# The first, the batch-change and the last steps of a pipelined fp32 block kernel in another order

## The reference

```python
x = x + layernorm(attn(layernorm(x)))     # long convolution, out projection, gated MLP
x = x + layernorm(ffn(layernorm(x)))      # two layers with weights changed per batch
# attn, its last part
y = (yconv + xv * D_skip) * x2
y = y @ out_proj_w.T + u
zm = rmsnorm(y, post_norm_w)
return y + gelu_tanh(zm @ l1_w.T) * (zm @ l2_w.T) @ l3_w.T       # 672 wide
# ffn: rows 1 to 16 of the batch make rank-one updates m1, m2 of W1 and W2
h = gelu(x @ W1.T + scale * (x @ m1.T) + b1)                     # 1024 wide
return h @ W2.T + scale * (h @ m2.T) + b2
```

## Time and profile before

| | us |
|---|---|
| median of three runs | 1096.37 |
| the profiled execution | 1095.71 |
| its span | 1093.9 |
| PE busy | 1063.1 (97% of the span) |
| DVE busy | 879.1 (80%) |
| ACT busy | 720.8 (66%) |
| POOL busy | 298.7 (27%) |

### The profile page before, as it was taken

How to read it: one execution, slowest core, us unless ns; L and a number is a source line. 1 busy time by engine, 2 the same in 40 slices (tenths; PEclk the granted TensorE clock), 3 DMA queues, 4 the chain that set the end, 5 groups by cost and what they waited for, 6 DMA issues and landing times.

```text
span 1093.9 us, 25039 instructions
## 1 busy us (share of the span) xinstructions
PE 1063.1 (97%) x9016; PEld 1007.7 (92%) x9016; DVE 879.1 (80%) x2313; ACT 720.8 (66%) x1613; POOL 298.7 (27%) x577
## 2 busy tenths in 40 slices
PE   8899999999999999999999999989999999999996
PEld 7777787778999999999999999989999999999996
DVE  7999998763788877888888777898888888877874
ACT  7878887664565666666666666665666666666553
POOL 6677784620001111112111111121112111111111
PEclk9999999999999999999999999999999999999999
DMA  3338988984642333333333333443333333333100
GB/s 127 117 126 229 270 229 219 400 312 59 147 73 40 59 60 49 59 49 50 52 55 63 56 59 49 109 105 50 50 59 49 51 53 57 65 59 49 31 11 30
DMA packets 113051, 104.93 MB, mean 96 GB/s; under 512 B 7600, under 2 KB 103792, under 8 KB 112672
## 3 DMA queue, kind: packets, MB, share of 16 engines
q1 hardware_dynamic: 111696, 100.77, 42.1%
q0 software_dynamic: 736, 2.51, 0.7%
q10 hardware_dynamic: 496, 0.05, 0.0%
HBM read 77.84 MB, written 32.80 MB: 101 GB/s over the span
## 4 chain that ended last, share of the span: by engine, by line
PE 63%; DVE 7%; issue 4%; POOL 1%; ACT 1%; DMA 0%; ACTq 0%; SPq 0%; DVEq 0%; POOLq 0%
PE ps_ring L1464 33%; PE ps_w L1464 14%; PE ps_m L1464 9%; PE ps_o L1464 4%; PE ps_rt L1479 2%; DVE base L1318 1%; POOL sc L1082 1%; DVE bn L1222 1%; PE ps_m L1529 1%; DVE prod L1265 0%; PE ps_w L1474 0%; DMA base<-in_w 0%; DVE ht_l L1234 0%; DVE pt_l L1234 0%; DVE x L1436 0%
## 5 line engine op out<-in xcount | busy, mean ns | idle before, releaser
L1082 POOL TENSOR_TENSOR sc<-sc,neg_half 128x2 f32<-128x2 f32 x128 | 95.5, 746 | 690.6 <-DVE sc L1417 407.8
L1142 ACT ACTIVATE gate<-ps_ring 128x256 f32<-128x256 f32 x192 | 73.0, 381 | 127.4 <-PE ps_ring L1464 126.6
L1163 ACT ACTIVATE hid<-ps_ring,b1s 128x256 f32<-128x256 f32 x256 | 112.4, 484 | 29.4 <-PE ps_ring L1464 9.3
L1464 PE MATMUL ps_ring<-mt_h,wl_h 128*128 128x256 f32 x640 | 125.8, 278 | 2.4 <-DVE prod L1265 1.3
L1464 PE MATMUL ps_ring<-mt_l,wl_h 128*128 128x256 f32 x640 | 125.7, 278 | 2.2 <-DVE mt_l L1234 2.2
L1464 PE MATMUL ps_ring<-mt_h,wl_l 128*128 128x256 f32 x640 | 125.0, 277 | 0.0
L1234 DVE TENSOR_TENSOR ht_l<-hid,ht_h 128x256 fp32r<-128x256 f32 x256 | 103.1, 423 | 16.0 <-ACT ht_h L1167 10.0
L1464 PE MATMUL ps_ring<-xt_h,we_h 128*128 128x256 f32 x512 | 103.2, 283 | 2.8 <-DVE prod L1265 2.4
L1265 DVE TENSOR_TENSOR prod<-ps_ring,gate 128x256 f32<-128x256 f32 x192 | 80.7, 420 | 24.9 <-ACT gate L1142 20.6
L1464 PEld LDWEIGHTS ps_ring<-mt_h,wl_h 128*128 128x128 f32 x640 | 96.6, 188 | 3.9 <-ACT mt_h L1211 2.2
L1464 PE MATMUL ps_ring<-xt_h,we_l 128*128 128x256 f32 x512 | 99.9, 276 | 0.0
(11 more groups left out here) (186 smaller groups left out, 2746.6 us busy)
## 6 DMA issues: line engine op xcount, KB each, us to landing
toep_scratch<-taps_scratch SPq DMA_DIRECT2D x30, 512.0 KB, 7.7
toep<-toep_scratch SPq DMA_DIRECT2D x30, 512.0 KB, 9.9
...
```

Source lines behind the costliest of these rows:

```text
L1082: nc.gpsimd.tensor_tensor(sc[:, to], sc[:, to], neg_half[:, 0, 0:CC], ALU.pow).then_inc(S[done], 1)
L1142: nc.scalar.activation(gate[rows_of, m % 2], ring[m % RING][rows_of, 0], ACT.Gelu_apprx_tanh).then_inc(S["gate_done"], 1)
L1163: nc.scalar.activation(hid[:, m % HIDS], block_of, ACT.Gelu, bias=b1s[:, m:m + 1]).then_inc(S["hid_done"], 1)
L1464: mm = nc.tensor.matmul(out, lhs(a, kk), rhs(b, kk), start=(j == 0), stop=(closed and j == len(todo) - 1))
```

## The change

The steps of the fill, of the batch change and of the end are put in another order on every engine:

- Unit 1's y and x2 are loaded at the start, into frow and hid, which are free then. DVE gates them at the end of step -1, ahead of step 0's products. PE runs unit 1's out projection behind the second block of step 0 and transposes its scaled rows ahead of step 0's `mlp_down`; ACT makes its squares and scaled rows between the gates. Unit 2's y is gated at the end of step 0, ahead of the sum of `mlp_down`.
- In steps 1 to 3, 18 and 19 (`relieved`) ACT makes the high parts of the fifth and sixth block and of the next unit's y, which DVE made before.
- Table loads are left out in steps 0 and 1, and come behind the high part of the transposed rows in steps -1, 2 and 18. The low part of the transposed rows comes sooner on DVE. The low parts of the last two pieces of the second weights move from one step's end into the next step's products.
- `mlp_down` is split, with `turn_scaled` between its halves in step 1. The tables of spare matmuls are smaller.
- SP loads the next batch's first weights ahead of the output's store.
- The last unit is finished in two chunks of 128 rows: each `ffn_down` half has its own PSUM tile and its own signal, the statistics, the power, one multiply-add and a store are made per chunk on DVE and POOL, without ACT. In the last two units `ffn_down` starts with six of the eight high parts there.

```diff
-    BEFORE_TURN = {0: (8, 7, 8, 6), 2: (0, 0, 0, 6), 3: (0, 5, 0, 4), 19: (0, 5, 5, 5)}
-    BEFORE_HIGH = {0: 9, 1: 10, 2: 10, 3: 9, 19: 9}
-    BEFORE_LOW = {1: 13, 2: 7, 3: 13, 19: 10}
-    BEFORE_DOWN = {0: (6, 6), 1: (4, 4)}
+    BEFORE_TURN = {0: (8, 7, 8, 6), 3: (0, 3, 0, 4), 19: (0, 5, 5, 5)}
+    BEFORE_HIGH = {0: 4, 3: 4, 19: 4}
+    BEFORE_DOWN = {0: (10, 7), 1: (0, 11)}
...
+        def bare(n):
+            return valid(n, UC) and not valid(n - FFN_AT, UC)
+        def exposed(n):
+            return bare(n) or (valid(n, UC) and late(n - FFN_AT))
+        def sooner(n):
+            return n == 1
+        def relieved(n):
+            return n in (1, 2, 3) or any(n == b * UCB + i for b in range(1, B) for i in (2, 3))
+        def highs(n):
+            return FB if relieved(n) else ACT_HIGHS
+        def highs_done(n, m):
+            return sum(highs(i) for i in range(n)) + m + 1
+        def highs_here(n, m):
+            return sum(FB - highs(i) for i in range(n)) + m - highs(n) + 1
+        def early(n):
+            return n == 2
+        def gated(n):
+            return hid[:, 0:KB] if sooner(n) else x2s[:]
...
+            load_y(1, frow, y_second)
+            sp.dma_start(gated(1), x2_dram[:, :, TC:2 * TC]).then_inc(x2_second, 16)
+            sp.wait_ge(S["yrow_done"], 1)
+            sp.dma_start(xa[:], x_rows[1]).then_inc(S["xa_in"], 16)
...
-                if valid(n + 2, UC):
-                    sp.wait_ge(S["yf_done"], n + 2)
-                    load_y(n + 2)
-                    sp.wait_ge(S["yl_done"], n + 2)
+                if valid(n + 2, UC) and not sooner(n + 2):
+                    last = 1 if sooner(n + 1) else n + 2
+                    sp.wait_ge(S["yf_done"], last)
+                    load_y(n + 2, yin, S["y_in"])
+                    sp.wait_ge(S["yl_done"], last)
...
+                if made:
+                    load_base1(made)
+                if w == LAST:
+                    for c in range(CC):
+                        sp.wait_ge(S["out_done"], w + c + 1)
+                        sp.dma_start(out_rows[w][:, c], xa[:, c]).then_inc(S["rows_out"], 16)
...
+                if m == FULL:
+                    nc.scalar.activation(pstack[REST:2 * REST], src, ACT.Copy).then_inc(S["stacked"], 1)
...
-                        if 0 < m < FB - 1:
+                        if 0 < m <= highs(n):
                             product_high(n, m - 1)
-                        if n == 0 and m == 3:
+                        if m == 2 and relieved(n) and valid(n + 1, UC) and not early(n + 1):
+                            gated_high(n + 1)
...
+                        if second is not None and m == 1:
+                            high_parts(second, (LORA + 1,))
                         if m in (2, 3) and valid(w, UC) and not late(w):
                             last_norm(w, m - 2)
-                    load_table(ACT.Gelu)
+                        if sooner(n + 1) and m == 2:
+                            squares(n + 1)
+                        if sooner(n + 1) and m == 4:
+                            scaled_rows(n + 1)
+                    if relieved(n):
+                        product_high(n, FULL)
+                    if valid(h, UC):
...
+                    if not sooner(n + 1):
+                        squares(n + 1)
+                        scaled_rows(n + 1)
+                    if valid(n, UC) and not exposed(n):
+                        load_table(ACT.Gelu_apprx_tanh)
...
+                    if not valid(n, UC) or (exposed(n) and not bare(n)):
+                        load_table(ACT.Gelu_apprx_tanh)
...
+            def last_chunks(w):
+                kept = x1[:, w % KEPT]
+                dve.wait_ge(S["a_mean"], w + 1)
+                for c in range(CC):
+                    nc.vector.tensor_scalar(kept[:, c], kept[:, c], mean_a[:, w % KEPT, c:c + 1], None, ALU.subtract
+                                            ).then_inc(S["x_bare"], 1)
+                for c, bank in enumerate((ps_w, ps_m)):
+                    dve.wait_ge(S["w2_mm"], w + c + 1)
+                    nc.vector.tensor_tensor(xa[:, c], bank[:, c], b2s[:], ALU.add).then_inc(S["f_done"], 1)
+                    dve.wait_ge(S["f_done"], w + c + 1)
+                    nc.vector.bn_stats(bn[:, 2, c], xa[:, c]).then_inc(S["f_stat"], 1)
+                    stats = 2 * (CC * w + c) + 1
+                    aggregate_after(dve, nc.vector, mark[:], S["f_stat"], stats)
+                    nc.vector.bn_aggr(mvf[:, c], bn[:, 2, c]).then_inc(S["f_stat"], 1)
+                    dve.wait_ge(S["f_stat"], stats + 1)
+                    nc.vector.tensor_scalar(sc[:, 2, c:c + 1], mvf[:, c, 1:2], EPS_LN, None, ALU.add
+                                            ).then_inc(S["f_var"], 1)
+                    nc.vector.tensor_scalar(xa[:, c], xa[:, c], mvf[:, c, 0:1], None, ALU.subtract
+                                            ).then_inc(S["f_bare"], 1)
+                    dve.wait_ge(S["f_bare"], c + 1)
+                    dve.wait_ge(S["x_bare"], CC)
+                    dve.wait_ge(S["f_scale"], w + c + 1)
+                    nc.vector.scalar_tensor_tensor(xa[:, c], xa[:, c], sc[:, 2, c:c + 1], kept[:, c],
+                                                   ALU.mult, ALU.add).then_inc(S["out_done"], 1)
...
+                if bare(n):
+                    turned_low(n + 1)
+                if early(n + 2):
+                    for part in range(3):
+                        gate_y(n + 2, part)
...
+                    if exposed(n) and not bare(n):
+                        turned_low(n + 1)
...
+                    if made == 0:
+                        up_weights(made, LORA // 2)
+                    elif made is not None:
+                        turned_low(n + 1)
+                    if first is not None:
+                        down_weights(first, LORA + 1, range(1))
...
+                    down_weights(first, LORA + 1, range(1, LORA))
...
+                if second is not None:
+                    low_part(second, LORA, "weight_low2")
...
+                if second is not None:
+                    low_part(second, LORA + 1, "weight_low2")
...
+                bank = ps_m if (h, c) == (LAST, CC - 1) else ps_w
+                highs_ready = ()
                 if c == 0:
-                    pe.wait_ge(S["hh_even"], HB // 2 * (h + 1))
-                    pe.wait_ge(S["hh_odd"], HB // 2 * (h + 1))
+                    behind = (HB - HIGHS_FIRST) // 2 if h >= LAST - 1 else 0
+                    pe.wait_ge(S["hh_even"], HB // 2 * (h + 1) - behind)
+                    pe.wait_ge(S["hh_odd"], HB // 2 * (h + 1) - behind)
+                    if behind:
+                        highs_ready = ((S["hh_even"], HB // 2 * (h + 1)), (S["hh_odd"], HB // 2 * (h + 1)))
...
+                        if sooner(n + 1) and m == 1:
+                            out_projection(n + 1)
+                    if sooner(n + 1):
+                        turn_scaled(n + 1)
...
+                if valid(u, UC) and bare(n):
+                    turn_second(u)
                 if valid(n, UC):
-                    mlp_down(n)
+                    mlp_down(n, 0)
+                    if bare(n) and not sooner(n + 1):
+                        turn_scaled(n + 1)
+                    mlp_down(n, 1)
```

233 lines of the change are left out of this document (137 added, 96 removed).

## The result

The changed kernel takes 1101.58 us, the median of six runs (1099.26 to 1105.32), against 1096.55 us for the kernel before in the same comparison. The ratio is 1.0048, with a 95% interval of 1.0032 to 1.0064: slower by about 5 us, where 2.3 us less were forecast. The time is outside the range of the prediction. The profiled execution took 1103.78 us, its span is 1102.0.

A forecast was written before the change was run, and what follows sets the result against it. PE's matmuls bound the kernel between 400 and 680 us, so only fill, batch change and end could move: +1.9 + 0.2 − 4.4 = −2.3, from 1096.37 to 1094.1 us, range 1092.3 to 1096.0.

The forecast's parts named there:

- The end: From the last `ffn_down` to the finish: earlier starts and two chunks give −4.4 us, between −3.0 and −4.7.
- The earlier starts of `ffn_down`: Units 30 and 31: starting with six of eight high parts gains 0.75 us each time, 1.5 together.
- The halved store: At the end: a half's store takes as long as the whole's, 2.6 us; by size alone 1.3 more gained.
- the 0.9 that I kept open: At the end: up to 0.9 us less gain if POOL's power waits behind DVE's subtraction; 0.69 taken for the power.
- The fill: Up to unit 0's `ffn_down`: it starts at 345.8 against 343.84 us, +1.9, bounds −0.5 to +3.5.
- The batch change: Up to unit 16's `ffn_down`: it starts at 746.8 against 746.58 us, +0.2, between −1 and +1.5.
- as far from unit 0's as before less 1.7: Trace sign at the batch change: unit 16's `ffn_down` follows unit 0's by the earlier 402.7 us less 1.7.
- rival 3: PE idles near 2 us in four fill places, fewer spare matmuls; a clock fall costs 5.7 us: 1099.8 us, chance 0.06.
- two signs of being wrong: Wrong if unit 0's `ffn_down` starts before 343.8 us, or if the last chunk takes more than 4 us.
- Rival 1: Early gating pays: fill −0.5, batch change −0.5, end −4.4, giving 1091.0 us; chance 0.27.
- rival 4: The edits cancel out in the fill: fill 0, the change −4.2, giving 1092.2 us; chance 0.07.
- Rival 2: The end gives little, 2.0 us instead of 4.4, since its chunks' chains are serial on DVE: 1096.5 us; chance 0.10.

The follow-up runs named there:

- e_spare: The changed kernel with 96 more spare matmuls in front of PE's long new waits; 1098.11 us, ratio 0.9996 to the kernel before.
- e_old_end: The changed kernel with the end of the kernel before, so fill and batch change alone; 1104.87 us, ratio 1.0066 to the kernel before.
- e_copies_batch: As e_spare, with the copies back on DVE only in steps 18 and 19, without 14 spare matmuls for unit 16; 1095.71 us, ratio 0.9989.
- e_few_spare: The kernel before with fewer spare matmuls and nothing else changed; 1100.01 us, ratio 1.0030 to the kernel before.
- e_copies_only: The changed kernel with the copies back on DVE and no spare matmuls added; 1096.29 us, ratio 0.9996 to the kernel before.
- e_copies_dve: The changed kernel with the copies back on DVE and 68 spare matmuls added in PE's waits; 1093.00 us, ratio 0.9960 to the kernel before.
- e_gate_dve: As e_copies_dve, with unit 2's y gated in step 1 as before, 18 spare matmuls replacing 28 at another place; 1092.71 us, ratio 0.9969.

## Why the prediction was wrong

**The end (−4.4).** Right in kind, and nearly in size: 2.0 to 3.5 by the ratios, 3.3 to 3.9 by the medians, 3.9 by the trace. (The sum itself, 1091.32 less 1087.0, is 4.3.) The two parts were off against each other. The earlier starts of `ffn_down` gave 0.3 and 0.6 us instead of 0.75 each, and unit 31's gave 0.37 back in front of the last high part. The chunk's chain took 2.6 us (2.7 forecast), with 0.59 for the power. The halved store ended 2.1 us after the last multiply-add instead of 2.6, so 0.5 us sooner than the sum had it; so the two ways to price it, by size or not at all, bracket what was measured. The Trainium skill, "DMA: Bandwidth & Descriptors", section "Anatomy of one DMA", has a fixed part of some 2 us for DMAs that GpSimd issues; these stores are the sync engine's, and their 2.1 us are close to it. The power overlaps DVE's subtraction by 0.2 us and took 0.59 for one column, less than the 0.69 for two in the earlier trace rows, so that the 0.9 that I kept open by the Trainium skill's "Advanced Engine Details and Errata", Pool engine, wasn't charged. That page, section "GPSIMD Details", has the conflict only with DVE instructions in a 2-port mode or with two SBUF inputs, a condition that I had left out. The trace of before agrees: the power of 1.60 us ran beside the low parts we_l, which read two tensors, and the subtraction reads one.

**The fill (+1.9).** Nearly right in size: +2.5 in e_spare and +2.2 in e_old_end, two kernels with this order and no fall of the clock ahead of 345 us. In e_spare, with 0.35 added for its earlier start, the late marks are: first hid at 323.0 (forecast 323.1), yrow of unit 3 at 328.8 (328.9), mt_l at 334.1 (334.0), `ffn_down` at 346.3 (345.8). Part of that is luck. The marks ahead of them came sooner than forecast, unit 1's first product at 294.0 (295.1), xa_c of unit 3 at 309.3 (311.6), unit 2's first product at 312.2 (313.1), and from there to the first hid it took 10.8 us instead of 10.0. DVE's rows of it:

```profile
286.94 0.69 DVE L1339 TENSOR_TENSOR x2s<-yin,x2s 128x512 f32<-128x512 f32 x1 [3.20 <-DMA x2s<-x_scratch]
...
328.47 0.68 DVE L1484 TENSOR_TENSOR yrow<-ps_o,xa_c 128x512 f32<-128x512 f32 x1
...
333.71 0.69 DVE L1320 TENSOR_TENSOR mt_l<-ps_rt,mt_h 128x512 fp32r<-128x512 f32 x1 [0.47 <-ACT mt_h L1295]
```

In the changed kernel the late marks, less its 1.54, are 325.2, 331.0, 336.2 and 348.6. The 2.2 us by which they are behind e_spare's are the late landing of x2 of unit 2, by which DVE's products were 2.1 to 2.3 late from unit 1's first one on; the fall at 299.6 adds nothing that can be seen at these marks. I had given PE's wait in the ring for that product 1 us and it was 3.74. Of the 2.8 between, PE was 1.6 sooner than forecast (`mlp_down` of step 0 ended at 287.4, less the 1.54, not 289.0) and the product 1.2 later, since x2 of unit 2 landed at 289.5 and not 288.5. That landing isn't steady: in e_spare, the same order, DVE waited for x2 until 286.94, 4.2 us sooner than in the changed kernel's 291.16, of which 1.9 is the later start.

**The batch change (+0.2).** Under-sized. From unit 14 to 16 e_spare takes 1.3 us more than before, and with the copies back on DVE 0.5 less (e_copies_batch). I had the first hid 1.0 us later than before (723.5 against 722.46), with what the other edits give in it. From the last gate to hid the copies make 2.3 (1.90 us before, 4.19 in e_spare), since I left out what ACT waits for DVE's products, and behind unit 14's `ffn_down` the first hid comes 1.5 later. From mt_l to the last low part it was 12.2 us instead of 11.7. In the fill the same mistake was covered by the marks ahead of it, which came sooner. The mark "as far from unit 0's as before less 1.7" also contradicted my own sum, which had +0.2 there; the trace has +4.7 (402.74 to 407.48, the sum of three columns).

**The clock (rival 3, at 0.06).** This is the step that failed: the sum has the clock at nothing, and it is the largest part of the 7.5 us between forecast and measurement, 3.5 us by the medians and 5.7 by the ratios. I listed the four places in which PE would idle for near 2 us, saw that 63 spare matmuls had gone, and read the short idle times and the clock of 1.00 in the earlier trace rows as evidence against a fall. They were the spare matmuls' doing, and the change took those away. The price was also shaped wrongly. I had one fall of 5.7 us with all 48 matmuls of an `ffn_down` at half the speed; the traces have four or five, each at 0.50 for a bit over 3 us, which costs 1.6 us where PE is the bound (16.78 to 18.38 from unit 0 to 1) and nothing that can be seen at unit 0's `ffn_down` for the one at 299.6, where PE waits again before that point. Together it is 3.3 us in e_few_spare and, by the ratios, 5.7 in e_spare and 3.9 between e_copies_only and e_copies_dve. Neither of the two signs of being wrong that I had named looked at the clock, and neither came. A smaller step failed with it: the copies at the batch change, above.

**The other rivals.** Rival 1 (early gating pays) and rival 4 (the fill's edits cancel): e_gate_dve against e_copies_dve says that the gating is worth nothing. Rival 4 came true only with the copies taken out and the waits filled. Rival 2 (the end gives 2.0) was wrong by the traces and the medians; only the ratio of e_old_end to the changed kernel, with wide intervals, is as low as that.

**The sum, as measured.** By the ratios: −3.5 for the end, −0.9 for all other edits without copies and falls (0.9968 to 0.9960, within what can be told from none), and +9.7 for copies and clock together (0.9960 to 1.0048), which makes +5.3. Whichever of the two is mended first takes 5.7 away and the second 3.9. The intervals are 1 us and more to either side, so that the 1.8 that they share is likely rather than shown; the wait for hid, which the copies make and ahead of which nothing runs, is where they would share it.
